# State-space layer: the exponential of the softplus is added to its positive part by an adding DMA, and TensorE sums three tensors in place of four

## The reference, cut to what matters

```python
dt = jax.nn.softplus(dt @ W_dt.T + b_dt)      # (tokens, 384)
def step(h, inp):
    dt_t, B_t, C_t, x_t = inp
    dA = jnp.exp(dt_t[..., None] * A)
    h = dA * h + (dt_t * x_t)[..., None] * B_t[:, None, :]
    y = jnp.einsum('bdn,bn->bd', h, C_t)
```

## Time and profile before

| | |
|---|---|
| Median of 3 runs | 4942.9 us (4937.89 to 4946.77) |
| The profiled execution, its own time | 4934.78 us |
| Its span, first to last instruction | 4933.0 us |
| Mean granted TensorE clock | 0.957 of full |
| Busy in the span: PE, DVE, ACT, POOL | 90%, 70%, 48%, 65% |
| State-space loop in the span | about 1250 us to 3980 us |

### The profile page before, as it was taken

How to read it: one execution, slowest core, us unless ns; L and a number is a source line. 1 busy time by engine, 2 the same in 40 slices (tenths; PEclk the granted TensorE clock), 3 DMA queues, 4 the chain that set the end, 5 groups by cost and what they waited for, 6 DMA issues and landing times. The chain is left out here.

```text
span 4933.0 us, 62114 instructions
## 1 busy us (share of the span) xinstructions
PE 4431.2 (90%) x17128; PEld 2288.0 (46%) x17128; DVE 3453.2 (70%) x4958; ACT 2366.7 (48%) x3986; POOL 3229.0 (65%) x1657
## 2 busy tenths in 40 slices
PE   6999987996899999998989899999999877999993
PEld 4666644663334343343333344343434335666662
DVE  4766763111799999999999999999999975111114
ACT  2555542212566666665566566656566534222220
POOL 2222222441899999998989989999999932444441
PEclk9999997997999999999999999999999988999997
DMA  1000012331233233332223232323233211334335
GB/s 30 23 19 19 19 60 63 115 108 51 92 101 109 95 107 106 104 106 97 99 86 107 100 101 98 114 99 103 98 103 104 99 62 56 110 117 117 114 109 186
DMA packets 248101, 444.69 MB, mean 90 GB/s; under 512 B 37292, under 2 KB 162172, under 8 KB 247900
## 3 DMA queue, kind: packets, MB, share of 16 engines
q1 hardware_dynamic: 222556, 390.84, 24.4%
q0 software_dynamic: 25344, 51.94, 3.7%
HBM read 398.90 MB, written 43.78 MB: 90 GB/s over the span
## 5 line engine op out<-in xcount | busy, mean ns | idle before, releaser
L1688 POOL TENSOR_TENSOR m_xh<-m_u,m_Bb 128x1536 f32<-128x1536 f32 x512 | 1761.8, 3471 | 181.1 <-DVE m_u L1564 181.1
L1617 PE MATMUL bank<-m_xh,ident 128*128 128x512 f32 x3072 | 1444.6, 606 | 26.4 <-POOL m_xh L1677 26.4
L1644 ACT ACTIVATE bank<-m_dt,m_Ac 128x508 f32<-128x508 f32 x1536 | 1021.0, 683 | 474.8 <-DVE bank L1659 320.3
L1659 DVE TENSOR_TENSOR_SCAN bank<-bank,m_xh 128x512 f32<-128x512 f32 x864 | 1059.7, 1227 | 34.0 <-ACT bank L1644 7.8
L1617 PEld LDWEIGHTS bank<-m_xh,ident 128*128 128x128 f32 x3072 | 569.1, 192 | 806.3 <-issue 730.9
L1677 POOL TENSOR_TENSOR m_xh<-m_xh,m_Cb 128x1536 f32<-128x1536 f32 x224 | 773.7, 3454 | 8.8 <-DVE m_xh L1659 8.8
L1659 DVE TENSOR_TENSOR_SCAN m_xh<-bank,m_xh 128x512 f32<-128x512 f32 x672 | 771.1, 1201 | 6.6 <-POOL m_xh L1688 3.6
L1668 DVE TENSOR_TENSOR m_xh<-bank,m_Cb 128x512 f32<-128x512 f32 x864 | 597.2, 691 | 68.2 <-DMA m_Cb<-BC_rows 23.0
L1143 ACT ACTIVATE f1t_h<-bank,f1t_b 128x512 f32<-128x512 f32 x234 | 148.2, 684 | 549.6 <-PE bank L1173 549.6
L1075 POOL DMA_INDIRECT rows_y<-f1t_y,f1t_home x156 | 153.7, 985 | 338.5 <-DVE f1t_y L1113 302.9
L1478 PE MATMUL bank<-m_xp,m_dg 128*128 128x512 f32 x768 | 349.6, 597 | 3.3 <-ACT m_xc L1486 2.6
(11 more groups left out here) (333 smaller groups left out, 6217.2 us busy)
## 6 DMA issues: line engine op xcount, KB each, us to landing
m_Bb<-BC_rows SPq DMA_DIRECT2D x256, 512.0 KB, 4.7
m_Cb<-BC_rows SPq DMA_DIRECT2D x256, 512.0 KB, 3.9
f1t_w<-f_w SPq DMA_DIRECT2D x39, 576.0 KB
f1t_w1a<-f_w SPq DMA_DIRECT2D x39, 384.0 KB
f1c_yg<-rows_y SPq DMA_DIRECT2D x16, 768.0 KB, 8.3
f0t_w<-f_w SPq DMA_DIRECT2D x19, 576.0 KB
f1t_w1b<-f_w SPq DMA_DIRECT2D x78, 96.0 KB
f0t_w1a<-f_w SPq DMA_DIRECT2D x19, 384.0 KB
```

Source lines behind the costliest of these rows:

```text
L1617: mm = pe.matmul(bank[:, c, :], K.ident[:, :], xh[n % NX][:, c, :], start=False, stop=(d == 1 and n == NS - 1))
L1644: act.activation(o[:, :, lo:hi], seqs(dt[d][:, c, :])[:, :, lo:hi], ACT.Exp, scale=Ac[:, c, n:n + 1]).then_inc(s_dA, 1)
L1659: dve.tensor_tensor_scan(o, bank[:, 3 + p % 3, way], xh[n % NX][:, c, way], 0.0, ALU.mult, ALU.add).then_inc(s_h, 1)
L1688: pool.tensor_tensor(xh[n % NX][:, :, :], u[d][:, :, :], Bb[q % RB][:, n % QN, :].unsqueeze(1).to_broadcast([P, DC, TOK]), ALU.mult).then_ ...
```

## The change

POOL gets a new step. It waits for exp(-|x|), then issues a DMA from SBUF to SBUF that adds `e[d]` to `r`. PE waits for that DMA before the first block of the softplus sum, and sums r, 1 - w1 and lw, three calls to a block. POOL's step stands at unit 28 in half 1 and at unit 33 in half 0.

```diff
+            "pool_add": (28, 33)
+        s_er, = ctx.software(K, 1)
...
+            def pool_add(pool):
+                pool.wait_ge(s_e, s + 1)
+                stand_alone(pool, K.go)
+                pool.dma_start(r[:, :, :].rearrange("p c t -> p (c t)"), e[d][:, :, :].rearrange("p c t -> p (c t)"),
+                               accum_op=ALU.add).then_inc(s_er, 16)
+
             def pe_sp(pe, c):
                 if c == 0:
+                    pe.wait_ge(s_er, (s + 1) * 16)
+                    stand_alone(pe, K.go)
                     pe.wait_ge(s_nc, s + 1)
                 elif not first:
                     pe.wait_ge(s_u, s * DC + c)
-                for k, t in enumerate((r, e[d], w1[d], lw)):
-                    mm = pe.matmul(bank[:, front(c), :], K.ident[:, :], t[:, c, :], start=(k == 0), stop=(k == 3))
+                for k, t in enumerate((r, w1[d], lw)):
+                    mm = pe.matmul(bank[:, front(c), :], K.ident[:, :], t[:, c, :], start=(k == 0), stop=(k == 2))
                 mm.then_inc(s_spps, 1)
...
+            put("pool", POS["pool_add"][d], pool_add)
```

More of the change, by code:

```diff
@@ L1309, in mamba_phase @@
             "act_dt0": (22, 25, 27), "pe_dt1": (21, 25, 26), "act_dt1": (27, 28, 30), "pe_pj": (18, 20), "act_pj": (20, 25),
-            "act_xc": (19, 22), "act_e": (27, 32), "act_w1": (30, 34), "act_ln": (31, 35), "pe_sp0": (31, 36, 41),
+            "act_xc": (19, 22), "act_e": (27, 32), "pool_add": (28, 33), "act_w1": (30, 34), "act_ln": (31, 35), "pe_sp0": (31, 36, 41),
             "act_sp0": (36, 41, 42), "u0": (35, 39, 42), "pe_sp1": (38, 40, 42), "act_sp1": (39, 42, 43), "u1": (38, 40, 42),
```

## The result

The changed kernel takes 5048.3 us in the median (5010.4 to 5081.2, 4 runs), the kernel before 4944.8 us (4937.9 to 4949.4, 4 runs). The ratio is 1.021, with a 95% interval of 1.012 to 1.029. The change makes the kernel slower, by about 2%. Executions more than 1.5% above the fastest of their kernel (five of the 60 of the kernel before that were taken beside the experiments, one of e2) are left out of all ratios, medians and ranges here.

The account below looks back on a forecast made before the run. The prediction took POOL's products plus its wait for DVE's third u to bound a half. Half 0's 67, half 1's 80 and the clock's 40 us made +187 us on 4935, 5122, so 5130 us for the median; range 4980 to 5290 us.

Parts of the forecast that it names:

- The mechanism: State-space halves: POOL waits for DVE's third u; PE's softplus sum starts at the DMA's landing; POOL's issue costs nothing.
- L0 - 3.7 and L1 - 5.2 us: Change in length of half 0 and half 1, from landing times L0 and L1: 4.2 and 5.3 us.
- the length L: Adding DMA's time from issue to landing: L0 = 7.9 us in half 0, L1 = 10.5 us in half 1.
- The chain ahead of the loop: Work before the loop: the change costs nothing there, within 3 us.
- The clock: PE restarts at the low clock after idling: one and a half slow calls, 1.3 us a half, 40 us in all.
- The worth of the calls: Calls removed from PE's softplus sum: gain of 1.9 us in half 0, at most 3.3 us in half 1.
- rival (c): The DMA lands fast, 3.3 us in both halves, and the kernel gets faster: 4910 us; chance 0.07.
- (a): The adding DMA costs as a plain copy, 2.8 us of engine time: 5020 us; chance 0.19.
- (b): The adding DMA costs two reads or more, 5.6 us of engine time: 5230 us; chance 0.27.
- (d): Gains and losses meet in the middle, landing near 4.4 us: within 10 us of before; chance 0.05.
- The side effect: Norm's sums on DVE that run long: more or fewer of them, some 14 us each, range wider by 30 us both sides.
- What the profile was to show: PE waits 6 and 8 to 11 us, POOL idle some 330 us, landing 8 to 10 us, 576 matmul records.

Follow-up runs that it names:

- e2: Changed kernel with the same adding DMA, but PE sums four tensors without reading r or waiting for it; ACT waits instead: 4954.4 us, ratio 1.001.
- e6: Kernel before with the norm's sum on DVE moved from unit 15 to unit 22: 4905.7 us, ratio 0.992.
- e7: Changed kernel with the norm's sum on DVE moved from unit 15 to unit 22: 5036.5 us, ratio 1.017.
- e1: Kernel before with three calls to a block and no DMA, 1 - w1 left out of the sum: 4907.2 us, ratio 0.993.
- e11: Kernel before with three calls to a block, no DMA, 1 - w1 left out, and the norm's sum at unit 22: 4869.3 us.
- e3: Changed kernel with a plain copy of e over r in place of the addition: 4945.4 us, ratio 1.001.
- e9: Changed kernel with the norm's sum at unit 22 and POOL's step at unit 25 in place of 28 in half 1: 4988.2 us.
- e12: e9 with idle calls on PE during the wait, 5 in half 1 and 3 in half 0: 4938.3 us.
- e5: Changed kernel with idle PE calls during the wait for the DMA, 8 in half 1 and 2 in half 0: 5029.6 us, ratio 1.016.

## Why the prediction was right, and which terms were off

**The mechanism** was right: POOL's wait for the third `u` ties the halves together, PE's start of the sum moved from the end of 1 - w1 to the landing, POOL's issue (listed with 0.84 us against the 1 us taken; the next product starts 0.6 to 0.7 us after it) and its wait for e cost nothing (e2), and PE then idled long enough to restart low. The formula of the prediction, L0 - 3.7 and L1 - 5.2 us, holds with the time measured from issue to PE's start: 6.0 - 3.7 = 2.3 us, measured 87.9 - 85.9 = 2.0; 8.1 - 5.2 = 2.9 us plus 2.6 us of clock, measured 86.5 - 81.1 = 5.4. The sums that free the `xh` buffers were to come "not before the third `u`"; in halves 0 they end 0.09 us behind it, still too early to hold POOL.

One reading on the way was loose: 79.7 us of products and the 2.8 us wait make 82.5 us, more than the 81.1 us of half 1. Listed lengths overlap. Products start 3.40 us apart, which gives 78.2 + 2.8 = 81.0 us; in half 0 the norm's statistics and the wait for them come on top. The forecast does not hang on it.

**The step that was mis-sized is the length L**, "L0 = 7.9" and "L1 = 10.5 us"; it measured 6.0 and 8.1 to PE's start. The engine time of the addition, 4.2 us, was near the 4.0 us measured, but by luck: the copy was taken as 2.8 us from the loads' 277 GB/s and is 2.0 us, and three streams for two was taken as the factor where it is two. What failed is what was put around it. From issue to first byte and from last byte to PE it is 1.5 and 0.5 us and not 1.6 and 0.7; and in half 0 the sharing with the next two loads, counted at 1.4 us, did not happen, because those loads were issued 4.4 us after the addition and its last bytes were through when theirs came. In half 1 sharing cost 2.1 us and not 4.2; the DMA records show some 550 to 690 KB of other transfers beside the addition there. By the sum this is 16 x 1.9 + 15 x 2.4 = 66 us too much. The chain ahead of the loop was put at "nothing, within 3 us" and cost 5 us; the DMA takes 10.6 us to land there.

**The clock** was taken at 1.3 us to a half. It is up to 2.6 us, in every half 1 and in 6 of 16 halves 0 of the profiled execution: 55 us and not 40.

With both corrected the sum is 187 - 66 + 15 = 136 us. This counts the clock as it fell with the norm's sum in its old place, where the price without the noise is 118 us; the 131 us of e6 and e7 hold nearly all halves 0 at the low clock. So some 20 us stay over: the first and last half 0 hardly changed, and the longer halves of the kernel before (87.5 and 82.2 us) were counted as if they were 85.9 and 81.1.

**The worth of the calls** was right only in the use that the sum made of it. When PE starts late, one call less brings the third `u` 2.1 and 3.2 us nearer to the start (12.5 and 17.2 us against 14.65 and 20.4), as taken. When PE starts on time, it brings 1.2 and 0.5 us (e1), or 1.3 and 0.9 us on average (e11 against e6), since DVE's scans fill the time. So rival (c) was too hopeful in half 1: it had 1.8 us there for a fast landing, and with no wait at all it is 0.9 us.

**The rivals.** (a), the copy's price, gave 5020 us with landings of 5.1 and 7.9 us and ended nearer than the forecast, for a wrong reason: its landings are off by 0.9 us and less, but the addition costs two copies. The 3.8 us that the prediction set beside rival (c) as an estimate is what the copy took in most halves 0 (3.6 to 4.1 us to land) and 2 us short for the addition (5.8 us). (b) was right in the factor of two and wrong in the size of a copy, so its 5230 us is out. (d) is where e3 stands.

**The side effect** of the long sums was named with its 14 us each and with 30 us to both sides. It was larger: the runs of the kernel before lay between 4903 and 4979 us over all the experiments, and the profiled pair differs by 76 us where its price without long sums is 118.

**What the profile was to show.** Right: 576 records (3 x 192), the wait named by the DMA on `r`, 0.84 us of issue, and the wait of 8.3 to 10.5 us in half 1 (8 to 11 was said). Off: the wait in half 0 is 2.3 to 4.1 us in most (6 was said); POOL's idle time grew to 228 and not 330 us; the landing's median is 6.7 us and not 8 to 10; PE's busy time fell by 29.5 us only (4431.2 to 4401.7), since the calls that are left are listed longer where the clock is low (724, 697 and 682 ns on average in place of 626, 618 and 597).

## What to carry to other kernels

A call taken off an engine is worth what the next engine waits for it, not its length: here 0.86 us per block gave 0.2 to 0.4 us, close to the waits before `u` in the profile before. A transfer put in place of a product must be priced by issue, first byte, bytes and what else is under way when it is issued, and placed by the loads around it; 3.4 us earlier helped in one half and hurt in the other. And when the runs of a kernel lie in steps, look for the instruction whose length comes in two sizes and take it out before a small effect is measured.

## What the runs showed of the hardware

An adding DMA from SBUF to SBUF of 768 KB in float32 holds the 16 engines for 4.0 us at 193 GB/s, a copy for 2.0 us at some 393 GB/s. PE starts 6.0 us after the issue of the one and 4.0 us after the other when they have the engines to themselves; beside loads of 512 KB the addition takes 8 to 10 us. POOL's issue is listed with 0.84 us for the addition and 0.61 us for the copy; the next product starts 0.6 to 0.7 us after the issue with both.

After the issue of the addition POOL's next products are listed 0.1 to 0.25 us longer each (3.6 to 3.7 us in place of 3.45), until POOL next waits; after the copy's they are not. The distance of their starts stays 3.4 us in both. The cause was not tried.

DVE's sum with both inputs in SBUF takes 0.96 us alone, about 2 us when it gets in between two of POOL's products, and 15.7 us when it does not. A long case of the kernel before, with the last two products that it waited over:

```profile
2467.00 15.75 DVE L1396 TENSOR_TENSOR H<-H,m_z 128x768 f32 x1
...
2475.09 6.84 POOL L1688 TENSOR_TENSOR m_xh<-m_u,m_Bb 128x1536 f32<-128x1536 f32 x2
```

It started 2.1 us into a product, and four more followed without a gap; it ended 0.8 us after the last of them. Moved to where POOL stops, it was never long (e6, e7, e9 to e12). The Trainium skill, SBUF — State Buffer, section "Who interferes with whom", says that such a DVE instruction contends with a POOL instruction that reads SBUF. The trace agrees. But in the long cases the wait does not end with the POOL instruction that was running; it lasted over four more. What decides which of the two gets in at a boundary stays open: in the kernel before the long ones started 2.06 to 2.08 us into POOL's product and behind the same DVE instructions as the short ones, of which one started at 2.06 us as well.

Idle calls on PE made the sum behind them faster: eight calls of 0.86 us, whose result nobody reads, took 2.6 us off a half in eight of 15 halves 1 (e5), where the granted clock was 1.00, the 2.4 GHz level, over the sum; without them it was 0.50 during the wait. Placed with the earlier issue (e12 against e9), such calls took 50 us off the kernel.
